# An attention block with FP4 feed-forward layers on one core: Q and K of a head pair from split operands in two row tiles, V, PV and the projection in other quarters

## The reference

```python
x = x + 0.5 * ffn(layernorm(x))        # fp4-quantized gate, up, down; inner size 352
xm = layernorm(x)
q, k, v = (split_heads(xm @ w) for w in (w_q, w_k, w_v))   # 16 heads of 64
attn = softmax(einsum('bnqd,bnkd->bnqk', q, k) * 64 ** -0.5)
o = merge_heads(einsum('bnqk,bnkd->bnqd', attn, v))
y = o @ w_proj + b_proj + xm
x = x + layernorm(y) * gamma + beta
x = x + 0.5 * ffn(layernorm(x))
```

## Time and profile before

| | |
|---|---|
| median of 3 runs | 2265.52 us (2261.74 to 2266.74) |
| the profiled execution | 2263.16 us, span 2261.4 us |
| TensorE busy | 2142.7 us, 95% |
| VectorE busy | 1605.5 us, 71% |
| GpSimd busy | 1407.7 us, 62% |
| ScalarE busy | 1151.4 us, 51% |
| mean granted TensorE clock | 0.978 |

### The profile page before, as it was taken

The page is one execution under the profiler, slowest core; times in us unless marked ns, Lnnn a source line. Parts: engine busy times, 40 slices in busy tenths (PEclk is TensorE's granted clock), DMA queues, the critical chain, the costliest instruction groups (busy, mean ns, idle before and its releaser), DMA issues.

```text
span 2261.4 us, 38387 instructions
## 1 busy us (share of the span) xinstructions
PE 2142.7 (95%) x14537; PEld 1094.4 (48%) x14537; DVE 1605.5 (71%) x2609; ACT 1151.4 (51%) x1749; POOL 1407.7 (62%) x1289
## 2 busy tenths in 40 slices
PE   3899999999999999999999999999999999999974
PEld 2344444545445454545545454554544545454432
DVE  5565767767687786868777686877778687776634
ACT  2455554645555454555545455455555545454532
POOL 3365666757576675757756576675757667665642
PEclk8799999999999999999999999999999999999986
DMA  1000000000000000000000000000000000000000
GB/s 60 1 7 2 6 2 2 12 2 7 7 7 7 2 11 2 7 7 7 7 2 11 2 7 7 2 12 2 10 3 6 7 2 12 2 2 7 2 7 10
DMA packets 167493, 15.83 MB, mean 7 GB/s; under 512 B 148304, under 2 KB 166928, under 8 KB 167312
## 3 DMA queue, kind: packets, MB, share of 16 engines
q1 hardware_dynamic: 167312, 13.39, 5.1%
HBM read 7.03 MB, written 4.19 MB: 5 GB/s over the span
## 4 chain that ended last, share of the span: by engine, by line
PE 85%; DVE 6%; SPq 2%; issue 2%; POOL 2%; DMA 1%; ACT 1%; POOLq 0%; DVEq 0%
PE pS L934 23%; PE pO L961 20%; PE pM L918 9%; PE pX L946 5%; PE pM L1077 5%; PE pX L985 5%; PE pM L973 3%; PE LpF L333 2%; PE FpF L333 2%; SPq L568 2%; PE FpF L296 2%; PE LpF L296 2%; PE LpF L309 2%; PE FpF L309 2%; PE LpF L324 1%
## 5 line engine op out<-in xcount | busy, mean ns | idle before, releaser
L676 POOL TENSOR_TENSOR ES<-ES,E 128x512 f32<-128x512 f32 x512 | 654.9, 1300 | 217.1 <-ACT E L747 209.9
L747 ACT ACTIVATE E<-pS 128x1024 f32<-128x1024 f32 x512 | 523.2, 1022 | 459.9 <-PE pS L934 421.3
L799 DVE TENSOR_REDUCE nmax<-pX 128x2 fp32r<-128x1024 f32 x512 | 622.0, 1215 | 113.4 <-PE pX L946 98.4
L961 PE MATMUL pO<-E,VA 128*64 128x512 f32 x2048 | 552.3, 618 | 0.0
L670 POOL TENSOR_TENSOR ES<-E 128x512 f32<-128x512 f32 x256 | 321.9, 1279 | 247.5 <-ACT E L747 247.5
L918 PE MATMUL pM<-xf,w_raw 128*64 128x512 f32 x1024 | 267.1, 600 | 2.8 <-DVE QL L889 2.1
L934 PE MATMUL pS<-QH,KH 64*128 64x512 f32 x1024 | 255.9, 496 | 0.0
L946 PE MATMUL pX<-KH,QH 64*128 64x512 f32 x1024 | 241.0, 412 | 4.7 <-DVE nmax L799 3.3
L934 PEld LDWEIGHTS pS<-QH,KH 64*128 64x128 f32 x1024 | 95.5, 183 | 288.1 <-issue 269.3
L946 PEld LDWEIGHTS pX<-KH,QH 64*128 64x128 f32 x1024 | 186.3, 306 | 36.7 <-DVE nmax L799 8.0
L934 PE MATMUL pS<-SH,onesr 64*128 64x512 f32 x1024 | 203.6, 393 | 0.0
(11 more groups left out here) (178 smaller groups left out, 3000.0 us busy)
## 6 DMA issues: line engine op xcount, KB each, us to landing
RROW<-RC SPq DMA_DIRECT2D x512, 2.0 KB, 2.0
xin<-in_L_attn_x SPq DMA_DIRECT2D x16, 256.0 KB, 3.0
SH<-nmax SPq DMA_DIRECT2D x256, 2.0 KB, 2.0
LC<-LROW SPq DMA_DIRECT2D x256, 2.0 KB, 2.1
out<-X SPq DMA_DIRECT2D x16, 256.0 KB, 2.5
w_raw<-in_L_attn_w_q SPq DMA_DIRECT2D x1, 512.0 KB, 3.6
w_raw<-in_L_attn_w_k SPq DMA_DIRECT2D x1, 512.0 KB, 4.7
w_raw<-in_L_attn_w_v SPq DMA_DIRECT2D x1, 512.0 KB, 5.6
```

The costliest lines, as they stand in the source:

```text
L676: ins = g.tensor_tensor(ES[i % 3][:, hd, :], ES[i % 3][:, hd, :], E[s][:, hd, :], ALU.add)
L747: a.activation(E[s][:, :, :], pS[:, :, :], ACT.Exp).then_inc(s_exp, 1)
L799: v.tensor_reduce(nmax[px % 2][:, :, t:t + 1], pX[:, :, :], AX.X, ALU.max, negate=True).then_inc(s_max, 1)
L961: ins = pe_.matmul(pO[half(hd), :], VA[of][:, kt, j * 128 + 64 * hd:j * 128 + 64 * hd + 64], E[kt][:, hd, :], start=kt == 0, stop=kt == KT ...
```

## The change

Q and K of pair i + 2 are computed together in quarter 1, from operands that are split beforehand into a high and a low fp32r part: `W` (once, from raw weights that are loaded into `E[0]` and `E[1]`) and `xs` (once a batch). `query_key` runs in two turns. In turn 0, rows 0 to 63 of the array give half of Q into `pM` and rows 64 to 127 half of K into `pO`; in turn 1 the sides are exchanged. Each turn is six matmuls; the second waits for the first (`s_side`), and `for_maxima` stands between them. V keeps an fp32 copy `xf` and its own weights `wv`; its round moves from quarter 3 to quarter 0 (seven of eight; one is at quarter 3 of p 0, none in p 5). PV parts 0 and 1 both come in quarter 2, and part 0 waits for `KL`, which reads `pO`. The projection stays in quarter 1, which now has no PV. `QH`, `QL`, `KH`, `KL` and `OT` have three buffers instead of four, `xf` one instead of two, and the layers' `xm` is dropped for `xn`.

```diff
+    def v_place(r):
+        c, k = r // 8, r % 8
+        p, s = ((-2, 0), (-1, 0), (0, 0), (0, 3), (1, 0), (2, 0), (3, 0), (4, 0))[k]
+        return PAIRS * c + p, 3 if c == 0 and k < 2 else s
...
-                        a.activation(xf[c % 2][:, :], F.pF[:, :], ACT.Copy).then_inc(s_xf, 1)
+                        a.activation(xs[0][:, :], F.pF[:, :], ACT.Copy)
+                        a.activation(xf[:, :], F.pF[:, :], ACT.Copy).then_inc(s_xf, 1)
...
                         if s == 0 and there(i - 1, NP):
                             act.wait_ge(s_pv, 4 * i)
-                            wait(act, s_norm, i - 4)
-                            a.activation(OT[(p - 1) % 4][:, :], pO[:, :], ACT.Copy).then_inc(s_ot, 1)
-                        if s == 0 and there(i + 2, NP):
-                            act.wait_ge(s_q, i + 3)
-                            a.activation(QH[(p + 2) % 4][:, :], pM[:, :], ACT.Copy, scale=SCALE).then_inc(s_qhi, 1)
+                            wait(act, s_norm, i - 3)
+                            a.activation(OT[(i - 1) % 3][:, :], pO[:, :], ACT.Copy).then_inc(s_ot, 1)
                         if s == 1 and there(i + 2, NP):
-                            act.wait_ge(s_k, i + 3)
-                            a.activation(KH[(p + 2) % 4][:, :], pM[:, :], ACT.Copy).then_inc(s_khi, 1)
+                            act.wait_ge(s_qk, i + 3)
+                            a.activation(QH[(i + 2) % 3][:, :], pM[:, :], ACT.Copy, scale=SCALE).then_inc(s_qhi, 1)
+                            a.activation(KH[(i + 2) % 3][:, :], pO[:, :], ACT.Copy).then_inc(s_khi, 1)
...
+                        dve.wait_ge(s_xf, c + 1)
+                        v.tensor_tensor(xs[1][:, :], F.pF[:, :], xs[0][:, :].bitcast(F32), ALU.subtract).then_inc(s_xlo, 1)
...
-                        if s == 0 and there(i + 2, NP):
+                        if s == 1 and there(i + 2, NP):
                             dve.wait_ge(s_qhi, i + 3)
...
                             dve.wait_ge(s_khi, i + 3)
-                            v.scalar_tensor_tensor(KL[(p + 2) % 4][:, :], pM[:, :], 1.0, KH[(p + 2) % 4][:, :].bitcast(F32),
+                            v.scalar_tensor_tensor(KL[(i + 2) % 3][:, :], pO[:, :], 1.0, KH[(i + 2) % 3][:, :].bitcast(F32),
...
-                def per_head(k, p, x):
-                    for hd in range(2):
-                        ins = pe_.matmul(pM[half(hd), :], w_raw[:, k, p * 128 + 64 * hd:p * 128 + 64 * hd + 64], x,
-                                         start=True, stop=True)
-                    return ins
+                def query_key(i, p, turn):
+                    cols = slice(p * 128, p * 128 + 128)
+                    if turn == 1:
+                        pe.wait_ge(s_side, i + 1)
+                    for n, (w, x) in enumerate(((0, 0), (0, 1), (1, 0))):
+                        for side in range(2):
+                            k = (side + turn) % 2
+                            ins = pe_.matmul((pM, pO)[k][:, :], W[w][half(side), k, cols], xs[x][half(side), :],
+                                             start=turn == 0 and n == 0, stop=turn == 1 and n == 2)
+                    ins.then_inc(s_side if turn == 0 else s_qk, 1)
...
                         if kt == 0:
                             wait(pe, s_ot, i)
+                            pe.wait_ge(s_klo, min(i + 3, NP))
...
+                        if s == 1 and there(i + 2, NP):
+                            if p == 6:
+                                pe.wait_ge(s_xlo, b + 2)
...
+                            wait(pe, s_va, rounds_until(i, 0))
+                            wait(pe, s_ot, i)
+                            query_key(i + 2, (p + 2) % PAIRS, 0)
                         if s < 2:
                             for_maxima(i + 1, p + 1, s + 2)
                         else:
                             for_maxima(i + 2, p + 2, s - 2)
+                        if s == 1 and there(i + 2, NP):
+                            query_key(i + 2, (p + 2) % PAIRS, 1)
                         if s == 0:
                             times_v(i - 1, (p - 1) % PAIRS, KT - 1)
-                        else:
-                            times_v(i, p, s - 1)
+                        if s == 2:
+                            times_v(i, p, 0)
+                            times_v(i, p, 1)
+                        if s == 3:
+                            times_v(i, p, 2)
```

More of the change, by code:

```diff
@@ L428, in steps, with rounds_until @@
                 body(b, p, b % 2)
+    def v_place(r):
+        c, k = r // 8, r % 8
+        p, s = ((-2, 0), (-1, 0), (0, 0), (0, 3), (1, 0), (2, 0), (3, 0), (4, 0))[k]
+        return PAIRS * c + p, 3 if c == 0 and k < 2 else s
     def rounds_at(i, s):
[L432 to L441, removed]
+        return [r for r in range(max(i - 8, 0), min(i + 9, ROUNDS)) if v_place(r) == (i, s)]
+    def rounds_until(i, s):
+        return sum(v_place(r) <= (i, s) for r in range(ROUNDS))
     with ExitStack() as scope:
@@ L451, in make_program @@
         wdT = m.sb("wdT", [128, FT, D])
-        w_raw = m.sb("w_raw", [128, 3, NH * HD])
+        wv = m.sb("wv", [128, NH * HD])
+        W = [m.sb(f"W{k}", [128, 2, NH * HD], F32R) for k in ("hi", "lo")]
         wp = m.sb("wp", [128, PAIRS, D])
@@ L461, in make_program @@
         X2 = [m.sb(f"X2{i}", [128, T * D]) for i in range(2)]
[L462 to L466, removed]
+        xf = m.sb("xf", [128, S])
+        xs = [m.sb(f"xs{k}", [128, S], F32R) for k in ("hi", "lo")]
+        QH = [m.sb(f"QH{i}", [128, S], F32R) for i in range(3)]
+        QL = [m.sb(f"QL{i}", [128, S], F32R) for i in range(3)]
+        KH = [m.sb(f"KH{i}", [128, S], F32R) for i in range(3)]
+        KL = [m.sb(f"KL{i}", [128, S], F32R) for i in range(3)]
         SH = [m.sb(f"SH{i}", [128, S], F32R) for i in range(2)]
@@ L470, in make_program @@
         ES = [m.sb(f"ES{i}", [128, 2, S]) for i in range(3)]
-        OT = [m.sb(f"OT{i}", [128, S]) for i in range(4)]
+        OT = [m.sb(f"OT{i}", [128, S]) for i in range(3)]
         ON = [m.sb(f"ON{i}", [128, S]) for i in range(2)]
@@ L512, in make_program @@
         s_out = m.sem("s_out")
-        s_q = m.sem("s_q")
-        s_k = m.sem("s_k")
+        s_side = m.sem("s_side")
+        s_qk = m.sem("s_qk")
         s_v = m.sem("s_v")
@@ L539, in make_program @@
         s_yacc = m.sem("s_yacc")
+        raw = [E[k][:, :, :].rearrange("p h n -> p (h n)") for k in range(2)]
         with nc.Block() as block:
@@ L715, in first_ffn @@
                         F.act_magic_h(act, c, k)
+                    for c in batch_at(FirstLayer, FirstLayer.down, b, t):
+                        if c == 0:
+                            act.wait_ge(s_raw, 48)
+                            for k in range(2):
+                                a.activation(W[0][:, k, :], raw[k], ACT.Copy).then_inc(s_whi, 1)
                     for c in batch_at(FirstLayer, FirstLayer.apply, b, t):
                         wait(act, s_y0, c)
-                        norm_x1.apply(nc, act, c, F.xm, X1[c % 3])
+                        norm_x1.apply(nc, act, c, F.xn, X1[c % 3])
                     for c in batch_at(FirstLayer, FirstLayer.apply_x, b, t):
@@ L822, in first_ffn @@
                 def first_ffn(b, t):
+                    for c in batch_at(FirstLayer, FirstLayer.xf, b, t):
+                        dve.wait_ge(s_xf, c + 1)
+                        v.tensor_tensor(xs[1][:, :], F.pF[:, :], xs[0][:, :].bitcast(F32), ALU.subtract).then_inc(s_xlo, 1)
+                    for c in batch_at(FirstLayer, FirstLayer.down, b, t):
+                        if c == 0:
+                            for k in range(2):
+                                dve.wait_ge(s_whi, k + 1)
+                                v.tensor_tensor(W[1][:, k, :], raw[k], W[0][:, k, :].bitcast(F32), ALU.subtract).then_inc(s_wlo, 1)
                     for c, k in parts_at(FirstLayer, FirstLayer.max_h, b, t):
@@ L992, in first_ffn @@
                     for c in batch_at(FirstLayer, FirstLayer.turn_x, b, t):
-                        wait(pe, s_xf, c)
+                        wait(pe, s_xlo, c)
                         F.pe_x(pe, c)
@@ L1066, in body @@
                         for r in rounds_at(i, s):
-                            kt, of, xb = round_place(i, p, bpar, r)
-                            pe.wait_ge(s_klo, min(i + 3, NP))
+                            kt, of = r % 4, (r // 4) % 2
                             wait(pe, s_va, r)
-                            if there(i - 3, NP):
-                                pe.wait_ge(s_norm, i - 2)
-                            elif i == 2:
+                            pe.wait_ge(s_qlo, i + 3 if s == 3 else i + 2)
+                            wait(pe, s_norm, i - 2 if s == 3 else i - 3)
+                            if i == 3:
                                 pe.wait_ge(s_lrow, 1)
-                            if p == 5:
+                            if p == 6:
                                 pe.wait_ge(s_xf, b + 2)
```

(4 more changed lines are left out.)

57 lines of the change are left out of this document (24 added, 33 removed).

## The result

| | before | after |
|---|---|---|
| median, us | 2264.39 (2259.17 to 2266.74) | 2272.49 (2272.17 to 2275.91) |
| ratio to before | | 1.0044, 95% interval 1.0028 to 1.0060 |
| profiled execution: time, span | 2263.16, 2261.4 | 2272.31, 2270.5 |
| TensorE busy | 2142.7 (95%) | 2112.6 (93%) |
| us per batch, mean of eight in the middle | 133.33 | 134.28 |

The change makes the kernel 0.4% slower, 8 us; 40 were forecast. The sign and most of the waits came out. What failed is the size of two terms, the own wait and the projection at p 3, and what the sum left out.

The account below looks back on a forecast made before the run. TensorE, busy 95% of the span, was taken as the bound. Per batch -1.34 (sixteen times, -21 us) and +4.10 (some fifteen batches, +61) gave +40: 2263 to 2303 us, 1.7% slower; own range 2286 to 2328, stated range 2228 to 2328.

Parts of the forecast that it names:

- own wait: Second half of the Q/K block waits for TensorE's own signal: 0.25 us a pair, +2.0 a batch, range 0 to 2.5.
- projection at p 3: Projection waits for the maxima whose bank it takes: 0.47 us at p 3 against 0.70 before, net -0.23 a batch.
- matmuls and mode changes: Q and K from split fp32r operands instead of fp32: -2.56 us a batch; fewer row/column tile changes: -0.78.
- drain for `KL` at p 2, 6, 4: First PV in the third quarter waits for `KL`: 0.97 us each at p 2 and 6, 0.30 at p 4, +2.24 together.
- fourth quarter without V: Without V only PV covers the VectorE and ScalarE chains there: waits at p 0, 1, 2, 5, 6, +2.78 us a batch.
- V on `ON`, two late M steps: V's fourth-quarter wait for `ON` and two maxima steps' losses at p 2 go away: -0.69 us a batch.
- rival C: Backlog adds up, half a microsecond more in each of 64 late fourth-quarter handoffs: +32, 2335 us; chance 0.09.
- Rival A: Fourth-quarter waits and TensorE's own wait do not come out, as VectorE and ScalarE run ahead: 2231 us, faster; chance 0.27.
- Head and first batches: At the head a K projection that waited 1.42 us goes, two copies come; nothing taken, 3 us either way.
- B: Only TensorE's wait for its own signal is free: +8, 2271 us; chance 0.17.
- D: Split products do not overlap in the two row tiles: +177, about 2480 us; chance 0.02.
- five signs: Late PV at p 2 and 6, M after p 1, scores after p 6; TensorE busy some 50 less; second half 0.2-0.3 late.

Follow-up runs that it names:

- fp32 run: Changed kernel's order, but Q and K as two fp32 projections in column halves from unsplit weights: 2319.19 us, ratio 1.0224 to the changed kernel.
- no own wait: Changed kernel without exchanging array sides between the two Q/K turns, so the second needs no wait; half the products made twice: 2264.98 us, ratio 0.9991.
- K first: Changed kernel with K copied and subtracted ahead of Q on ScalarE and VectorE: 2258.9 us, ratio 0.9958 to the changed kernel.
- rounding step: Changed kernel with V back in the fourth quarter, K copied ahead of Q, and one VectorE rounding step a slot later at p 3: 2224.42 us, ratio 0.9831.
- V late: Changed kernel with V back in the fourth quarter of every pair, nothing else: 2249.64 us, ratio 0.9913 to the changed kernel.
- both repairs: Changed kernel with V back in the fourth quarter and K copied and subtracted ahead of Q: 2228.07 us, ratio 0.9853 to the changed kernel.
- adjacent: Changed kernel with the second Q/K turn straight behind the first and the maxima products behind both, wait kept: 2361.31 us, ratio 1.0440.
- adjacent_no_own: Changed kernel with both Q/K turns back to back, maxima products behind, sides not exchanged and no wait between turns: 2320.18 us, ratio 1.0253.

## Why the forecast went wrong, point by point

Each term in us a batch. "Measured" is from start to start in the batch above, or from the experiment named.

| step of the forecast | forecast | measured | shown by |
|---|---|---|---|
| matmuls and mode changes | -3.34 | about -3.3 | trace (the block with its M takes 1.81 instead of 2.04 at p 0, 1.72 instead of 2.14 at p 2, own wait in it); the total of the fp32 run, in part by luck |
| own wait | +2.0 | +0.45 | no own wait |
| drain for `KL` at p 2, 6, 4 | +2.24 | +2.36 (1.01, 1.01, 0.34) | trace; K first takes 1.10 of it |
| projection at p 3 | -0.23 | +0.6 | trace; rounding step |
| fourth quarter without V | +2.78 | +2.46 | trace; V late (1.73 of it net, with the projection and the clock against it) |
| V on `ON`, two late M steps | -0.69 | -0.2 against the short batch, -0.7 against the mean | trace |
| not in the forecast | 0 | -0.6 and -0.4 | trace |
| sum | +2.76 | +1.4 against the short batch, +0.9 against the mean | |
| the batches themselves | | +1.19 and +0.95 | trace |

- **The own wait was mis-sized**, by 1.55 a batch, 25 us; the forecast is off by 30, and the other errors (projection +13, not in the forecast -16, fourth quarter -5, drain +2) nearly cancel. Two things failed. The row taken as nearest, is a step whose two loads take 0.34 together; here they take 0.18 each and run side by side. So the next pair comes 0.40 behind the end of the one waited for and not 0.60, and the term is 0.10 to 0.12 a pair where 0.25 was taken (0.31 at most). Bare it costs 0.34, and M, which stands beside it, covers 0.23 of that. And at odd p what is left falls where the projection waits for M's maxima in any case.
- **The Trainium skill's rule**, in "TensorE: Matmul & The Clock Gate", section Part 2, that weight loads are pulled ahead of matmuls in flight, did not carry past this wait: in both fences above the loads start 0.06 to 0.07 after the last matmul of the first turn ends, not under it. That it would make this term near nothing came close in time (7.5 us, not 0 and not 32), by another way: M stands beside the loads.
- **The projection at p 3 was mis-sized**, by 0.83, 13 us. The forecast took the maxima of M as free to start 0.43 after M, as at p 0. VectorE was already late there in the earlier trace rows, and a list for the second layer (`Lqh`, 0.87 and 1.25) and the rounding step (1.70 and 0.89) stand ahead of them. This was the backlog of rival C, at one place and not at 64.
- **The drain for `KL`** and **the fourth quarter** held, place by place, within 0.13. Rival A's reason against itself (each chain starts at a matmul just before, so idle time elsewhere does not help) is what V late and K first show: 1.73 a batch comes back with V, and 1.09 more with K first.
- **What the sum left out**: small waits in the kernel before that the new order covers (0.24 at p 7, a gate step behind PV; 0.21 at p 1, the projection behind late maxima; 0.17 at p 3, V behind `ON` in the short batch; 0.62 in all), and two PVs in a row, which take 1.77 and not 1.82, 0.4 a batch. Both are read from the traces alone; no experiment parts them.
- **Head and first batches**: nothing was taken. In the two profiled executions the kernel after is 0.5 us ahead at the first projection and 2.8 ahead two batches later; only then it loses by the rate above. So 0.95 by sixteen, 15 us, is 8 in the median. Of the 2.3 us gained in these two batches some 1.5 are a fall of the granted clock to 0.50 for 3.4 us at 294.13, which the profile before has behind a wait of V (2.07 us) and the one after has not (estimate: half of the 3.1 us that TensorE worked in it). Why the rest goes the other way stays open.
- **Rivals.** A (2231) fell: the waits are there. B (2271) gave the nearest time and the nearest reason: the own wait is almost free. That it comes within 2 us is luck, since the projection (+13) and the steps left out (-16) nearly cancel. D fell at first sight: the pairs start 0.23 apart, as in the earlier trace rows.
- **What would show it**: of the five signs three are there as written (PV 2.27 behind the block at p 2 and 6, M late behind the maxima after p 1, scores waiting for the exponential after p 6), and two at half the size. The first pair of the second turn is late by 0.10, not 0.2 to 0.3. TensorE's busy time fell by 30 and not 50: a stalled pair's matmuls are recorded longer (0.62 instead of 0.40), and with both repairs, which take those waits away, it is 2095.7, 47 less than before.

## What to carry to other kernels

A faster form of a matmul and its new place in the order are two changes with two prices: here 47 us gained and some 55 lost, and moving only V back made the kernel 0.9% faster than before, V and K first 1.5%. On the bounding engine a step is also the cover of the chains that start at the step before it: write down, for every step that leaves a quarter, which chain it hid and what that chain's length is. And a wait that a trace doesn't show is best priced by two experiments, bare and in place; the price in place here was a third of the bare one.

## What the runs showed of the hardware

- Weight loads behind a semaphore wait start after the release: in all 256 blocks of the kernel after and of `adjacent` the first load of the second turn starts 0.06 us or more after the last matmul of the first turn ends. The two 64-row loads of a released pair run in both row halves at the same time (0.18 each, starts 0.01 apart), where the pair in the earlier trace rows takes 0.34; the weights there are read with a stride, here they are contiguous, and no run parts whether that is the reason. TensorE's wait for its own matmul costs 0.34 us bare and 0.10 to 0.11 with an M beside it.
- Twelve fp32r matmuls of 64 rows by 128 columns by 512, two at a time, take 1.39 us; the same Q and K as fp32 matmuls in column halves take 1.77.
- VectorE's `TENSOR_SCALAR` on 44 columns took 0.19 at 1018.06, with GpSimd idle, and 0.74 at 1042.82 and 1.25 at 1048.46, each beside a GpSimd operation of 2.5 us; a rounding step of 704 columns took 0.97 and 1.70 in the same batch. No experiment parted what makes the difference.
- In five places in the middle of these profiles the granted clock falls to 0.50 for 3.4 us right behind a wait of the projection at p 3 (2.24, 2.31 and 2.39 us in V late, 1.97 without the own wait, 1.90 with both repairs), and the steps in it take 1.5 to 1.8 us longer. Waits of 2.36 (V late) and 1.88 (`adjacent_no_own`) had none behind them.
